# A short tile of 84 rows is loaded with two transfers, of 80 and of 4 rows, in place of one

## The reference

```python
entities = jnp.einsum('be,le->bl', entity_idxs, W)     # (1024, 12500) x (128, 12500)
s = jnp.sum(entity_idxs, axis=1)
scale = jnp.where(s != 0, 1.0 / jnp.where(s != 0, s, 1.0), 1.0)
return entities * scale[:, None]
```

## Time and profile before

| | |
|---|---|
| median of 3 runs | 148.46 us (148.4 to 148.49) |
| the profiled execution | 148.27 us |
| its span (first to last instruction) | 146.5 us |
| what lies around the span | 1.8 us |
| PE busy | 135.3 us, 92% of the span |
| DVE busy, ACT busy | 95.0 us, 87.8 us |
| read from memory | 57.60 MB, 397 GB/s over the span |
| share of the 16 DMA engines' span taken by the transfers' packets | 95.2% |

### The profile page before, as it was taken

How to read it: one execution, slowest core, us unless ns; L and a number is a source line. 1 busy time by engine, 2 the same in 40 slices (tenths; PEclk the granted TensorE clock), 3 DMA queues, 4 the chain that set the end, 5 groups by cost and what they waited for, 6 DMA issues and landing times.

```text
span 146.5 us, 2384 instructions
## 1 busy us (share of the span) xinstructions
PE 135.3 (92%) x785; PEld 77.5 (53%) x785; DVE 95.0 (65%) x129; ACT 87.8 (60%) x152; POOL 0.5 (0%) x10
## 2 busy tenths in 40 slices
PE   0598999999999999989999999999999999999980
PEld 0223555655555556545656556556556556566540
DVE  0188626629927599472489956667592939578694
ACT  3188525618826588462478855556481928568782
POOL 1000000000000000000000000000000000000000
PEclk9999999999999999999999999999999999999999
DMA  5999999999999999999999999999999999999822
GB/s 158 401 430 433 452 423 413 442 428 413 448 428 411 425 438 427 433 443 413 422 423 423 430 429 430 427 422 415 433 413 433 415 410 414 412 406 402 319 80 72
DMA packets 7303, 58.18 MB, mean 397 GB/s; under 512 B 814, under 2 KB 1582, under 8 KB 3842
## 3 DMA queue, kind: packets, MB, share of 16 engines
q1 hardware_dynamic: 7298, 58.13, 95.2%
HBM read 57.60 MB, written 0.52 MB: 397 GB/s over the span
## 4 chain that ended last, share of the span: by engine, by line
DMA 43%; PE 40%; DVE 7%; SPq 6%; issue 2%; DVEq 0%; POOLq 0%
PE acc L434 40%; DMA xw<-loop 33%; DMA x_final<-ends 10%; SPq L221 4%; DVE low_max L339 3%; DVE y_sum L380 2%; SPq L219 1%; DVE w_rest L329 1%; DVE row_sum L377 0%; SPq L210 0%; SPq L211 0%; DVE row_sum L374 0%; DVE row_sum L371 0%; DVE any_low L412 0%; PE acc L476 0%
## 5 line engine op out<-in xcount | busy, mean ns | idle before, releaser
L434 PE MATMUL acc<-parts,xw 128*128 128x385 bf16 x720 | 121.8, 332 | 1.6 <-POOLq L206 1.2
L434 PEld LDWEIGHTS acc<-parts,xw 128*128 128x128 bf16 x720 | 70.6, 99 | 53.0 <-POOLq L206 5.0
L339 DVE TENSOR_REDUCE low_max<-xw 128x1536 uint16 x30 | 52.3, 1744 | 0.0
L280 ACT ACTIVATE act_out<-xw 128x1536 bf16<-128x1536 uint16 x30 | 44.0, 1467 | 0.0
L273 ACT ACTIVATE parts<-xw 128x384 bf16<-128x384 bf16 x30 | 15.7, 524 | 45.6 <-POOLq L206 45.6
L329 DVE TENSOR_TENSOR w_rest<-xw 128x384 f32<-128x384 f32 x30 | 16.7, 556 | 39.8 <-POOLq L206 39.7
L276 ACT ACTIVATE parts<-w_rest 128x384 bf16<-128x384 bf16 x31 | 16.3, 526 | 3.1 <-DVE w_rest L329 1.6
L335 DVE TENSOR_TENSOR parts<-w_rest 128x384 bf16<-128x384 f32 x31 | 17.4, 560 | 1.1
L434 PE MATMUL acc<-parts_short,xw_short 84*128 84x385 bf16 x8 | 2.7, 522 | 5.3 <-ACT parts_short L276 5.3
L280 ACT ACTIVATION_READ_ACCUMULATOR act_out<-xw x30 | 5.6, 187 | 0.0
L434 PE MATMUL acc<-parts_alone,x_final 128*128 128x385 bf16 x24 | 5.2, 326 | 0.0
(11 more groups left out here) (37 smaller groups left out, 14.7 us busy)
## 6 DMA issues: line engine op xcount, KB each, us to landing
xw<-loop SPq DMA_DIRECT2D x9, 2304.0 KB, 18.7
xw<-loop SPq DMA_DIRECT2D x10, 1728.0 KB, 19.0
xw<-loop SPq DMA_DIRECT2D x8, 1152.0 KB, 18.4
xw<-loop SPq DMA_DIRECT2D x8, 576.0 KB, 19.0
x_final<-ends SPq DMA_DIRECT2D x7, 384.0 KB, 15.3
xw_head<-ends SPq DMA_DIRECT2D x1, 960.0 KB, 6.3
out<-y SPq DMA_DIRECT2D x3, 128.0 KB, 1.7
xw_short<-ends SPq DMA_DIRECT2D x1, 378.0 KB
```

The costliest lines, as they stand in the source:

```text
L280: return nc.scalar.activation(tiles(act_out[0:rows, buf, 0:n * f], n), low(words), ACT.Copy, accum_out=low_max[0:rows, bass.ds(CHECKS + co ...
L339: return nc.vector.tensor_reduce(low_max[0:rows, bass.ds(col, 1)], low(words), AX.XY, ALU.max)
L434: return nc.tensor.matmul(acc[:, b, 0:N], x, parts, start=first, stop=last)
```

## The change

The short tile's 84 rows are issued as two transfers, of rows 0 to 79 (`EVEN = short // 16 * 16`, the multiple of 16 below 84) and of rows 80 to 83. Both add 16 to the same semaphore, and the three engines that wait for the short tile wait for 32 in place of 16. Everything else stays.

```diff
+    EVEN = short // 16 * 16
...
-            sp.dma_start(xw_short[0:short, :], edge(1)).then_inc(short_in, 16)
+            sp.dma_start(xw_short[0:EVEN, :], edge(1)[0:EVEN, :]).then_inc(short_in, 16)
+            sp.dma_start(xw_short[EVEN:short, :], edge(1)[EVEN:, :]).then_inc(short_in, 16)
             sp.dma_start(xw_head[:, :], edge(0)).then_inc(head_in, 16)
...
-            act.wait_ge(short_in, 16)
+            act.wait_ge(short_in, 32)
...
-            dve.wait_ge(short_in, 16)
+            dve.wait_ge(short_in, 32)
...
             pe.wait_ge(ones_set, 1)
-            pe.wait_ge(short_in, 16)
+            pe.wait_ge(short_in, 32)
```

More of the change, by code:

```diff
@@ L65, in rec_kernel @@
     FIRST_TILE = [sum(PIECES[:k]) for k in range(len(PIECES))]
-    assert 0 < short <= P and N < 512 and sum(PIECES) == LOOP and SLOTS % 2 == 0
+    assert 0 < EVEN < short <= P and N < 512 and sum(PIECES) == LOOP and SLOTS % 2 == 0
     assert all(a % RING + n <= RING for a, n in zip(FIRST_TILE, PIECES))
```

## The result

| | median | lowest to highest | runs |
|---|---|---|---|
| before | 148.43 us | 148.27 to 148.99 | 15 |
| changed | 149.41 us | 148.19 to 150.28 | 15 |

The ratio of the changed kernel to the one before is 1.006, 95% interval 1.0043 to 1.0077: 0.6 to 1.1 us more. The forecast was 148.55 us with a range to 149.1. The changed kernel's runs also spread over 2.1 us, those of before over 0.7. The profiled execution is one of the shorter ones, 148.54 us, 0.27 above that of before; a second profile of the same kernel (first experiment) took 149.93 us.

What follows compares the result with a forecast made beforehand. The prediction took the unbroken transfer stream, gated by its slowest DMA engine, as the bound. Stream +0.10, short tile's wait 0 and SP's hidden issue 0, added to the 148.46 us median, gave about 148.55 us, range 148.2 to 149.1.

Steps and rivals of the forecast that it cites:

- The count of DMA engines and reports (820): Short tile's load: 80 rows use 16 DMA engines and 4 rows use 4, so small packets go from 814 to 820.
- the wait for 32: Short tile's wait on ACT, DVE and PE: ends about when it does now, at worst 0.2 us later; cost 0.
- mainly the stream of transfers counts: Whole kernel: delaying the transfer stream's start reaches the end; delayed early compute doesn't if PE still waits for data afterwards.
- the added issue: SP's queue before the head: a third issue puts the head's issue at about 1.68 instead of 1.26, +0.42 us.
- +0.10, bounds -0.17 and +0.25: Head's start on the DMA engines: late arrival less the earlier end of five rows delays the stream +0.10 us.
- from the middle of the field: Head's start: the delay was taken for a DMA engine free before at 3.2 us, giving +0.10 us.
- its own reading of the earlier trace: Pieces near 72 us: the last DMA engine is over 1 us behind the pack, and every piece waits for it.
- the instruction packet near 27 us: One DMA engine near 27 us: a packet of instructions took 1.06 us, explaining a lag of that size.
- R1: Before the head: transfers are prepared one behind another, the head starts at 4.00, stream 0.8 us later, 149.3 us; chance 0.12.
- The forecast's own sign for R1: First piece in the changed profile: if it is 0.5 us late or more, slower one-behind-another preparation of transfers holds.
- R2: DMA stream: the slowest engine loses a row and its rank, together -0.37 us, 148.1 us; chance 0.12.
- R3: DMA stream: the instruction packet falls on the next-to-last engine, +0.85 us, 149.3 us; chance 0.06.

Runs made afterwards that it cites:

- first experiment: The changed kernel, unmodified, profiled and timed again against the kernel before: 149.48 us (148.99 to 149.93), ratio 1.0044.

## Why the forecast was wrong

*What held.* The count of DMA engines and reports (820), the head's issue at 1.61 (1.68 forecast), its first packet at 2.93 (forecast 2.9 to 3.3), and the wait for 32, which ended early. So did the reading that mainly the stream of transfers counts: a PE that began 3 us later cost 0.2 us by the medians.

*The step that failed* is the added issue, in the sum "+0.10, bounds -0.17 and +0.25". It let the head's rows come at one moment for all DMA engines and took that moment, less the end of the rows in front, for the loss. The measured term is +0.6 to +1.1 us. The head's first packet came in time (2.93). What came late is the head's work on single DMA engines: in six of the eight profiles of kernels with the head 0.3 to 0.5 us late, two to six engines report the first piece 0.5 to 2.6 us behind the others, differently in each. In the other two (84 rows with the wait; 48 and 32 rows) it isn't that: there less had flowed by 5 us (0.98 and 0.88 MB against 1.09 before). The forecast spoke of an engine "from the middle of the field", but a piece is complete with its last engine, which was its own reading of the earlier trace rows. That reading was itself half right: it put the two late engines of the earlier trace rows down to the instruction packet near 27 us, but one DMA engine is already over 1 us late at the first piece (the one report after 10.9, above), before that packet.

*The rivals.* R1 gave 149.3 us, near the result, by luck: the head's first packet, which it put at 4.00, came at 2.93, and three transfers in front of the head cost less than two. The forecast's own sign for R1, a first piece 0.5 us late or more, came true (0.55) all the same; it couldn't tell R1 from other ways of being late. R2 and R3 have a part of truth: an instruction packet falls on some DMA engine near 25 to 28 us in every kernel, and it can hit one that is already last or one that isn't. The run with 42 and 42 rows shows the first. At the first piece six engines are over 1 us behind the others. Near 74 us, 15 reports start in 72.5:75.0 and one in 75.0:76.0, which is 1.6 us after the one before it:

```profile
DMA packets 87, 1.06 MB, mean 422 GB/s; under 512 B 15, under 2 KB 15, under 8 KB 15
...
DMA packets 33, 0.45 MB, mean 447 GB/s; under 512 B 1, under 2 KB 1, under 8 KB 1
```

That execution took 150.67 us. Where no engine is late at the first piece (80 rows, 96, 128, 48 and 32, and the 4 rows first), one is 1.3 to 1.5 us behind the next near 72 us. That the packet makes this difference is argued from its time and its length, 1.06 us, not tested. So a late start of under about 1.3 us on an engine that the packet spares is hidden, and I take this for the reason why the profiled execution lost 0.55 us at the first piece and 0.27 at the end.

The profiled executions side by side:

| kernel | start of the first piece's matmuls | start of the matmuls after the piece near 74 us | execution |
|---|---|---|---|
| before | 11.77 | 73.91 | 148.27 us |
| changed | 12.32 | 74.18 | 148.54 |
| changed, again | 13.07 | 74.99 | 149.93 |
| 42 and 42 rows | 12.93 | 76.36 | 150.67 |
| 80 rows | 10.91 | 74.27 | 148.69 |
| 80 rows, wait | 12.73 | 74.62 | 148.99 |
| 84 rows, wait | 11.49 | 74.67 | 149.06 |
| 48 and 32 rows | 11.26 | 74.64 | 149.09 |
| 128 rows | 11.01 | 74.26 | 148.61 |
| 128 rows, wait | 13.46 | 75.31 | 149.62 |

The time follows the piece near 74 us, with 74.3 to 74.9 us more, and not the first piece. The run with 128 rows shows the same: its first piece was worked on at 11.01, 0.76 us earlier than before, yet the chain has

```profile
74.26 40.85 PE acc L434 x248
```

0.35 us later than before. Evening out the DMA engines' start is worth nothing here: 80, 96 and 128 rows in one transfer, on all 16, end between 0.9985 and 1.0 of the time before. One engine that is over 1 us late in the middle of the run explains it, and explains why the change had nothing to win.

*The cause, as far as it is shown.* A head issued 0.3 to 0.5 us later than before, with the first of the short tile's rows still issued at 0.75, loses 0.35 to 0.9% and scatters over 0.9 to 2.2 us: seven kernels, whether a transfer or a bare wait delays it, with 14 or 16 DMA engines, with five, six or eight rows in front. Issued at most 0.52 us behind the short tile's main rows it loses nothing clear of noise (before, and seven kernels with ratios of 0.9985 to 1.0014). Refuted as the cause are the spread over 16 DMA engines, the transfer on four engines, an added transfer as such (behind the head or on ACT's queue it costs nothing), and cover. That a transfer in front of the head costs more than a wait of the same length isn't excluded: two transfers for one lost 0.9% with 84 and with 128 rows, the wait 0.5 and 0.6%, and the intervals overlap. What fits most of them is that the head's issue has to be over before the main rows in front move. It ends at 1.61 to 1.63 us where nothing is lost and at 1.91 to 2.08 in the seven, and those rows first move at about 1.75 (at 2.13 with the 4 rows first, where the head's issue ends at 1.98). Two kernels don't fit its simple form: with the head at 2.06 (three transfers) no loss is clear of noise, and with the head at 2.00 the loss of 0.37% is there without the scatter. What happens inside a DMA engine that gets its second transfer just after it has begun its first stays open.

## What to carry to other kernels

Where a stream of transfers bounds a kernel, the first two microseconds of issue are part of it: add no issue and no wait between the first transfer and the next large one; a small piece that has to be split off can go behind them or on another engine's queue (ratios 1.0003, 0.9993 and 0.9997 here). Whether a kernel gains by a large transfer first on the same queue was not tried. Judge a transfer by its last DMA engine, not by the mean: count the reports (packets under 512 bytes) in a stretch before and after the pack. Do so at the transfer whose arrival sets the end, as well as at the first: here the first piece came 0.5 us earlier than before in a kernel that lost 0.35%. And where runs scatter more than those of before, one profile shows one draw: repeat the run before explaining its number.

## What the runs showed of the hardware

- A DMA engine's lag at the first piece was still there at 72 us: in the changed kernel's second profile five engines are late at 11 us, the last by 2.0 us (12.64 against a median of 10.64), and the same piece of the ring's load near 72 us has its last report 2.0 us behind the median again (74.43 against 72.41).
- One DMA engine can fall behind later: with 48 and 32 rows, 16 reports of 16 were in time at 10.9 us, and near 72 us one started 1.5 us after the other 15.
- In two profiles, with the head issued 0.36 us later, the first piece's matmuls started 1.8 us later (10.91 and 12.73), but the piece near 74 us only 0.35 us later.
- A short tile of 128 rows instead of 84, with 0.2 MB more to read, took the same time: 148.47 us, ratio 0.9994.
- Moving a transfer from SP's to ACT's queue isn't a free exchange: with the head on ACT's queue the short tile's matmuls began 1.77 us later (7.11 against 5.34), and the kernel took 0.28% longer.
